# Histogram of the sorting stage: the first key set's high one-hot rows move from VectorE to ScalarE

## The reference

```
row, col = (edge_index[0], edge_index[1])
msg = jnp.concatenate([x[row], edge_attr], axis=1)
h = jax.nn.elu(msg @ W1a + b1a) @ W1b + b1b
summed = jax.ops.segment_sum(h, col, num_segments=n)
counts = jax.ops.segment_sum(jnp.ones((h.shape[0],), dtype=h.dtype), col, num_segments=n)
agg = summed / jnp.maximum(counts, 1.0)[:, None]
z = jnp.concatenate([x, agg], axis=1)
return jax.nn.elu(z @ W2a + b2a) @ W2b + b2b
```

## Time and profile before

| | |
|---|---|
| median of 3 runs | 4410.17 us (4407.81 to 4410.22) |
| profiled execution: time, span | 4406.22 us, 4404.2 us |
| busy: PE, DVE, ACT, POOL | 79%, 76%, 52%, 69% of the span |
| mean granted TensorE clock | 0.924 |
| the stage in question | 36 to 162.5 us |

### The profile page before, as it was taken

One profiled execution on the slowest core, in us unless ns is written; L12 is line 12 of the kernel. 1 busy time (PEld: TensorE's weight loads), 2 busy tenths in 40 slices (PEclk: granted clock), 3 DMA queues, 4 the chain that ended last, 5 costly groups with the idle time before them and its releaser, 6 DMA issues. The chain is left out here.

```text
span 4404.2 us, 59487 instructions
## 1 busy us (share of the span) xinstructions
PE 3497.0 (79%) x14981; PEld 2181.8 (50%) x14981; DVE 3360.6 (76%) x10477; ACT 2304.7 (52%) x4672; POOL 3043.6 (69%) x2666
## 2 busy tenths in 40 slices
PE   5688888747776566499979999999699678687984
PEld 3466666624444566444435555555344367564331
DVE  6888888846666788655647888888688689787985
ACT  2498888713344577523337777777233222132752
POOL 1378888757775788677737888888577567463547
PEclk9999999979999788799989999999899889898997
DMA  3254445433332677444433443443344278694873
GB/s 86 92 146 140 138 142 148 124 98 91 96 96 75 187 203 207 143 131 143 137 116 105 133 132 125 133 132 116 106 129 133 77 233 253 142 194 132 278 235 119
DMA packets 463646, 621.80 MB, mean 141 GB/s; under 512 B 71541, under 2 KB 220204, under 8 KB 463308
## 3 DMA queue, kind: packets, MB, share of 16 engines
q1 hardware_dynamic: 402700, 534.09, 38.6%
q0 software_dynamic: 54912, 83.37, 9.0%
q10 hardware_dynamic: 5696, 0.55, 0.1%
HBM read 402.95 MB, written 218.46 MB: 141 GB/s over the span
## 5 line engine op out<-in xcount | busy, mean ns | idle before, releaser
L1195 PE MATMUL ps<-big,Whh 128*128 128x512 f32 x1176 | 537.4, 593 | 0.5 <-ACT big L1400 0.5
L1615 PE MATMUL ps<-big,We 128*128 128x512 f32 x800 | 355.5, 598 | 8.4 <-DVE big L1765 4.5
L1195 PEld LDWEIGHTS ps<-big,Whh 128*128 128x128 f32 x1176 | 212.9, 191 | 214.2 <-issue 211.4
L1228 POOL TENSOR_TENSOR big<-big 128x512 f32<-128x512 f32 x196 | 248.0, 1285 | 71.5 <-ACT big L1222 71.5
L604 POOL DMA_INDIRECT me<-node_tab,ix x208 | 239.7, 1152 | 70.8 <-issue 48.3
L611 POOL DMA_INDIRECT meta<-me,rank_ix x208 | 223.4, 1074 | 63.1 <-issue 60.5
L1765 DVE SCALAR_TENSOR_TENSOR big<-r2N,zN 128x512 f32<-128x512 f32 x400 | 254.0, 686 | 9.9 <-ACT zN L1676 6.2
L1213 DVE SCALAR_TENSOR_TENSOR big<-ps,bhh,hid 128x512 f32<-128x512 f32 x196 | 146.4, 747 | 141.2 <-ACT hid L1206 137.4
L1615 PEld LDWEIGHTS ps<-big,We 128*128 128x128 f32 x800 | 150.8, 191 | 195.1 <-issue 188.7
L688 PE MATMUL ps<-big,hotrow 128*128 128x256 f32 x832 | 201.5, 398 | 22.5 <-ACT hotrow L746 12.1
L1238 POOL TENSOR_TENSOR big<-big 128x512 f32<-128x512 f32 x98 | 141.5, 1464 | 109.1 <-DVE big L1233 109.1
(11 more groups left out here) (421 smaller groups left out, 11045.9 us busy)
## 6 DMA issues: line engine op xcount, KB each, us to landing
xN<-x_tab SPq DMA_DIRECT2D x196, 256.0 KB, 3.3
h_tab<-yN SPq DMA_DIRECT2D x124, 256.0 KB, 2.4
krow<-key_row SPq DMA_DIRECT2D x100, 256.5 KB, 4.4
agg<-in_xt SPq DMA_DIRECT2D x98, 256.0 KB, 3.3
big<-x_tab SPq DMA_DIRECT2D x98, 256.0 KB, 3.1
x_tab<-hid SPq DMA_DIRECT2D x98, 256.0 KB, 3.5
agg<-x_tab SPq DMA_DIRECT2D x98, 256.0 KB, 2.8
x_tab<-zN SPq DMA_DIRECT2D x98, 256.0 KB, 2.0
```

The costliest lines, as they stand in the source:

```text
L1195: last = nc.tensor.matmul(bank[:, :], Whh[:, l, c * D:(c + 1) * D], h, start=True, stop=not both)
L1228: nc.gpsimd.tensor_tensor(self.d[u], h[u], self.n[u], SUB).then_inc(self.dd, 1)
L1615: last = nc.tensor.matmul(MS[:, :], We[:, l * NTYPE + t, :], masked[g % 2][:, t, :], start=(t == 0), stop=(t == NTYPE - 1))
```

## The change

ScalarE gets a histogram step of its own. For k = 0 it makes the high rows as `hot_high` does: four Square, a wait for its own `squared_0`, one Relu, then `hist_hi`. VectorE's `hist` leaves these four rows out for k = 0 (`high` is true only for k = 1) and still makes the low rows of k = 0 and both kinds of k = 1. TensorE waits for `hist_hi` as well ahead of k = 0. The tiles stay the same single pair for each k, so ScalarE too waits for `histd` of step i - 1 (k = 0). In ScalarE's order the step stands where `plan` has it, two ahead of each dense step.

```
@@ tensor
                 def hist(i):
                     for k in range(2):
                         pe.wait_ge(hoth, 2 * i + k + 1)
+                        if k == 0:
+                            pe.wait_ge(hist_hi, i + 1)
@@ scalar
+                def hist(i):
+                    after(act, histd, 2 * (i - 1) if i else -1)
+                    hi = hots[0][1][0]
+                    for j in range(J):
+                        t = J * i + j
+                        last = nc.scalar.activation(hi[:, j, :], iota_lo[:, :], ACT.Square, bias=minus_hi[:, 0, t:t + 1])
+                    last.then_inc(squared_0, 1)
+                    act.wait_ge(squared_0, i + 1)
+                    nc.scalar.activation(hi, hi, ACT.Relu, scale=-1.0, bias=ones[:, 0:1]).then_inc(hist_hi, 1)
+
                 act.wait_ge(mv_set, 3)
-                follow(dense=dense, rank=rank)
+                follow(hist=hist, dense=dense, rank=rank)
@@ vector
                 def hist(i):
                     for k in range(2):
                         after(dve, histd, 2 * (i - 1) + k if i else -1)
-                        one_hots(i, k, 0, hoth)
+                        one_hots(i, k, 0, hoth, k == 1)
```

More of the change, by code:

```diff
@@ L476, in build @@
          hidd, reld, elud, xbd, y1d, r1d, st1d, mvd, epsd, powd, shd, x1d) = ph.sems(32)
-        tab_st, mv_set, squared, squared_hi, hot_hi, added = ph.sems(6)
+        tab_st, mv_set, squared, squared_hi, hot_hi, added, squared_0, hist_hi = ph.sems(8)
         rows_in, x_in, xt_in, o1 = ph.sems(2), ph.sems(3), ph.sems(4), ph.sems(3)
```

## The result

The changed kernel takes 4484.69 us in the median of four runs (4476.55 to 4492.70), the kernel before 4409.09. The ratio is 1.0171, with a 95% interval of 1.0152 to 1.0191: slower, by about 75 us. The profiled execution took 4476.55 us, its span is 4474.7.

A forecast was written before the change was run, and what follows sets the result against it. The prediction took VectorE to bound the histogram part, at 10.57 us a round; 45 us for the new ring, 26 for TensorE's clock and 1 for the table's matmuls gave 72 us, a forecast of 4481, range 4451 to 4503.

The forecast's parts named there:

- The new chain: Histogram rounds: added waits close a ring where ScalarE or TensorE works alone, 13.96 us a round against 10.57.
- 1. two turns and signals: Histogram round: ScalarE makes the k = 0 high rows twice, each with a 0.06 us signal to TensorE, 5.88 us.
- 2. first k = 0 matmuls: Histogram round: TensorE's first-step k = 0 matmuls and the signal back, 1.11 us, 0.8 longer at low clock.
- 3. second pair: Histogram round: TensorE's k = 0 and k = 1 matmuls of the second step, 1.76 us, 1.6 longer at low clock.
- +45 us at full clock: Histogram part: the longer rounds start the table at 207.9 in place of 162.48, with TensorE's clock full.
- +26 us for the clock: Histogram rounds: TensorE's clock falls once a round at the long gap, 2.4 us each, in 11 of 13 rounds.
- +1 us for the table's small matmuls: Table step: its two small matmuls stand behind a slower `hidden` and may hold VectorE 1 us.
- The sum: Whole kernel: 45 + 26 + 1 = 72 us on the profiled execution's 4406.2, so 4478; median forecast 4481.
- VectorE as the bound: Rival, histogram part: ScalarE makes rows ahead in idle time, rounds follow VectorE at 9.00 us, 4390; chance 0.04.
- The held clock: Rival, histogram part: the ring forms but TensorE's clock holds, +45 to +50, 4455 to 4460; chance 0.15.
- A mostly low clock: Rival, histogram part: the ring runs mostly at low clock, +90 to +110, 4500 to 4520; chance 0.13.
- the last rival: Rival, behind the table: part of the shift is taken back, between 0 and +40, 4410 to 4450; chance 0.06.

The follow-up runs named there:

- e1_fill: The changed kernel with harmless added matmuls on TensorE in its two gaps, 14 before odd and 32 before even steps' k = 0; 4456.59 us, ratio 1.0111.
- e9_swap: e4_lag_double with ScalarE's exps placed ahead of scale1 in the histogram rounds; 4394.97 us, ratio 0.9961.
- e7_apart: The changed kernel with ScalarE's turns writing a tile nobody reads and waiting for nobody, VectorE making all rows; 4410.16 us, ratio 0.9996.
- e5_odd: The changed kernel with ScalarE making the rows in odd steps only, VectorE making all rows in even steps; 4415.98 us, ratio 1.0012.
- e4_lag_double: The changed kernel with exps one group late in the histogram rounds and two tiles for the first key set's high rows; 4403.91 us, ratio 0.9992.
- e8_longer: The changed kernel with one more operation, a wait and a Square after the Relu, in each ScalarE turn; 4507.65 us, ratio 1.0215.

## Why the prediction was right

**The new chain: right, and shown part by part.** The parts in the round from 138.10 to 155.03, with the forecast at low clock where the clock was low:

| part of the ring | forecast, full clock + clock | measured |
|---|---|---|
| 1. two turns and signals | 5.88 | 3.04 + 3.02 = 6.06 |
| 2. first k = 0 matmuls | 1.11 + 0.8 | 1.90 |
| 3. second pair | 1.76 + 1.6 | 3.37 |
| 4. `out0` | 1.79 | 2.17 |
| 5. half of `hidden` | 1.14 | 1.14 |
| 6. `exps` | 2.28 | 2.29 |
| sum | 16.36 | 16.93 |

The turns' 3.03 us are 2.88 for the two operations, as the rank part had it, and 0.15 for the signal to TensorE (from the Relu's end at 143.28 to the matmul at 143.43). I had taken 0.06 from a signal of VectorE. That is 0.2 us a round.

**+45 us at full clock: measured 50.** e1_fill puts the store 50.0 us later with the clock held from 47 us on. Its table starts at 212.48 in place of 207.9, 4.6 us late. Between the first and the last `hidden` (47.94 to 213.40) it is 1.5 us longer than the sum forecast for these rounds, mainly the signals. The other 3.1 us are there already at the first `hidden`, which the sum has at 44.8. Of these 0.9 are the first turn, which I let start at 36.08; it waits for VectorE's `minus_hi` and starts at 37.01. The rest I put down to the low clock, which the trace has until 46.0 us, and to the added matmuls there, without a run of its own for it.

**+26 us for the clock: measured 24.6,** from e1_fill against the changed kernel. One fall a round was right, and so were the two places where it costs. Two small errors cancel here: I counted 11 rounds at 2.4 us, and the trace has fewer full ones but costlier. In all 13 rounds the first pair is slow, but the second only in 9 (the rounds are 13.0, 14.0, 14.5 and 14.9 us up to the fifth `hidden`), and in those a round costs up to 2.95 us more than in e1_fill, since `out0` too is caught for its first part. The Trainium skill ("TensorE: Matmul & The Clock Gate", "What's actually happening") says that activity releases the throttled state. The runs agree: filling the gaps with activity held 1.00 and gave 28 us of the medians back.

**+1 us for the table's small matmuls: wrong.** They were not held up. L663 starts at 241.24, 4.2 us after the table's first copy, as L661 did before (166.68 and 162.48), and waits 0.27 us for VectorE. That first copy is at 237.03, 3 us after the 234 that I gave: 4.6 us too little for the ring and 1.4 too much for the clock.

**The sum: right within the spread, with some luck.** On the profiled execution I had 72 us, and its time grew by 70.3; the median grew by 75.6 and stands 3.7 us above the 4481. The three errors, +4.6, -1.4 and -1, partly cancel. Among the signs, VectorE is busy 53% of the time up to the table (106.15 of 201.03 us), below the 60 to 70% that I gave, since the rounds are longer than at full clock; and TensorE's short gap is 1.36 us and not 2, since its k = 1 matmuls run at the low clock.

**The rivals.** VectorE as the bound, with 4390 us, needed a ring shorter than 9.00 us. e9_swap shows what that takes: three edits of ScalarE's order and tile, after which the time is 4394.97. The Trainium skill ("Perfetto Trace Analysis", "Optimizing Scalar/DVE Operations") says that offloading some of a saturated VectorE's work to ScalarE may make sense. That is right about the load, which e7_apart shows to fit; the section says nothing of the order. The held clock is the state of e1_fill, 4456.59 us, inside the 4455 to 4460 given for it. A mostly low clock did not come: the mean granted was 0.76. Nothing near what the last rival needed was taken back behind the table: the store's shift and the medians' agree within 1 us.

## What to carry to other kernels

Before moving work to an engine with idle time, follow each of the two new waits round once: if the producer's next turn is queued behind something that needs the consumer's result of this round, the turn's whole length stands in a ring, whatever the busy shares say. Add the ring up and compare it with the busiest engine's work: with two turns it was 14.1 us against 10.6 and set the round, with one (e5_odd) 10.0 and it did no harm while the clock held. Opening such a ring costs no more work, only order and a tile: let the producer run its other duty one group late, so that it does not wait for this round's result, and give it a second tile; then look for the next ring, which the first one hid. TensorE's idle time inside a ring has a second price in its clock, so count the gaps as well as the work.

## What the runs showed of the hardware

More TensorE work made the changed kernel faster: 46 added matmuls a round cut a round from 16.93 to 14.10 us, since the clock stayed at 1.00. A gap of 2.44 us was followed in e5_odd by a fall to 0.50, while one of 2.84 us, before the matmuls at 84.72, was not, so a ring with such gaps has rounds of 10.0 and of 12.9 us side by side. In e4_lag_double even 1.75 us of idle came before a fall, twice in its rounds, beside rounds with the same gap and none. So the length of the gap alone does not tell whether the clock falls. And the same gaps of 5.68 and 2.45 us in e8_longer left the second pair of matmuls at 3.22 us in one round and at 1.91 in another: the cost of a fall depends on where in the round it ends.
